# Self attention on one core: units per head, split values, weights streamed pair by pair, row sums inverted on GpSimd

## The reference, cut to what matters

```python
h = rmsnorm(layernorm(x)) * norm_w
q, k, v = h @ w_q, h @ w_k, h @ w_v          # 16 heads of 64
ll = where(tril, q @ k.T / 8, NEG)           # the window is the whole row block of 512
idx = top_k(h @ scorer_w + scorer_b, 128)
lg = where(idx <= pos, q @ k[idx].T / 8, NEG)
attn = softmax(concat([ll, lg]))             # a chosen key counts twice
out = x + (attn @ [v, v[idx]]) @ w_out
```

## Time and profile before

| what | value |
|---|---|
| median of 3 runs | 2299.57 us (2298.17 to 2301.93) |
| profiled execution, its own time | 2303.6 us |
| its span | 2301.9 us |
| mean granted TensorE clock | 0.945 |
| PE / PEld / DVE / ACT / POOL busy in the span | 92% / 72% / 57% / 40% / 15% |
| self attention | from the start to about 1560 us |

### The profile page before, as it was taken

One profiled execution on the slowest core, in us unless ns is written; L12 is line 12 of the kernel. 1 busy time (PEld: TensorE's weight loads), 2 busy tenths in 40 slices (PEclk: granted clock), 3 DMA queues, 4 the chain that ended last, 5 costly groups with the idle time before them and its releaser, 6 DMA issues. The chain is left out here.

```text
span 2301.9 us, 36078 instructions
## 1 busy us (share of the span) xinstructions
PE 2120.8 (92%) x12029; PEld 1654.5 (72%) x12029; DVE 1320.5 (57%) x3145; ACT 930.6 (40%) x1989; POOL 343.7 (15%) x605
## 2 busy tenths in 40 slices
PE   3999999999999999999999999996899999978899
PEld 2886787688588688778868868864788888854543
DVE  5584376178167347537717826743787878745401
ACT  3442344244144244334415414424866666413210
POOL 2100100010010010001001001003554445320000
PEclk9999999999999999999999999996987878769899
DMA  5000000100100100000010010002013212150000
GB/s 192 1 2 33 24 1 13 44 1 1 56 1 1 55 3 1 27 31 1 11 47 1 1 57 1 1 33 81 27 59 133 61 58 67 51 201 1 1 0 19
DMA packets 46137, 80.24 MB, mean 35 GB/s; under 512 B 10067, under 2 KB 10067, under 8 KB 45448
## 3 DMA queue, kind: packets, MB, share of 16 engines
q1 hardware_dynamic: 45320, 75.85, 9.9%
q0 software_dynamic: 640, 2.10, 0.2%
HBM read 60.11 MB, written 17.83 MB: 34 GB/s over the span
## 5 line engine op out<-in xcount | busy, mean ns | idle before, releaser
L403 ACT ACTIVATE probs<-s_bank,nmax 128x512 f32<-128x512 f32 (+3 forms) x512 | 249.5, 526 | 368.5 <-DVE nmax L534 266.4
L686 PE MATMUL o_bank<-vals,probs_t 128*128 128x65 f32 x2560 | 329.0, 272 | 0.1
L686 PEld LDWEIGHTS o_bank<-vals,probs_t 128*128 128x128 f32 x2560 | 312.5, 192 | 13.1 <-DVE probs_t L542 12.9
L534 DVE TENSOR_REDUCE nmax<-s_bank 128x1 f32<-128x512 f32 (+2 forms) x384 | 184.4, 508 | 189.2 <-PE s_bank L663 186.5
L710 PE MATMUL pj_bank<-w_o,o_t 128*128 128x512 f32 x512 | 221.8, 594 | 6.0 <-ACT o_t L411 6.0
L542 DVE COPY probs_t<-pt_bank 128x512 f32<-128x512 f32 x320 | 217.8, 681 | 2.2 <-PE pt_bank L671 2.1
L671 PE MATMUL pt_bank<-ident,probs 128*128 128x128 f32 x1280 | 194.9, 275 | 15.7 <-DVE o_t L449 15.7
L659 PE MATMUL s_bank<-k_twice,q_both 128*128 128x512 f32 (+3 forms) x512 | 190.0, 373 | 2.1 <-DVE k_lo L522 2.1
L710 PEld LDWEIGHTS pj_bank<-w_o,o_t 128*128 128x128 f32 x512 | 96.6, 190 | 126.5 <-issue 126.5
L381 ACT ACTIVATE vals<-pj_bank,twice 128x512 f32<-128x512 f32 x64 | 43.9, 688 | 340.4 <-PE pj_bank L583 334.8
L518 DVE SCALAR_TENSOR_TENSOR q_both<-pj_bank,q_both 64x512 fp32r<-64x512 f32 x128 | 88.1, 688 | 141.7 <-ACT q_both L390 139.1
(11 more groups left out here) (268 smaller groups left out, 4125.3 us busy)
## 6 DMA issues: line engine op xcount, KB each, us to landing
xb<-in_x SPq DMA_DIRECT2D x9, 1024.0 KB, 5.8
xt<-x SPq DMA_DIRECT2D x36, 256.0 KB, 2.8
probs<-in_x SPq DMA_DIRECT2D x32, 256.0 KB, 2.6
x<-probs SPq DMA_DIRECT2D x32, 256.0 KB, 2.0
am<-in_L_ffn_attention_mask SPq DMA_DIRECT2D x8, 1024.0 KB, 5.3
out<-x SPq DMA_DIRECT2D x32, 256.0 KB, 2.5
w_sb<-in_L_ffn_w SPq DMA_DIRECT2D x2, 4096.0 KB, 20.4
o_t<-in_L_attn_w_v SPq DMA_DIRECT2D x2, 1024.0 KB, 9.6
```

Of the source, the lines that this page charges most:

```text
L403: ins = nc.scalar.activation(probs[:, i % 2, c0:c0 + nk], s_bank[i % 2][:, c0:c0 + nk], ACT.Exp, bias=nmax[:, i % 4, n:n + 1])
L534: ins = nc.vector.tensor_reduce(nmax[:, i % 4, n:n + 1], s_bank[i % 2][:, c0:c0 + nk], AX.X, ALU.max, negate=True)
L686: ins = nc.tensor.matmul(o_bank[slot][:, o0:o0 + VW], probs_t[:, i % 2, c0 + P * kt:c0 + P * kt + P], vals[:, kt, 2 * p + h, :], start=(kt ...
```

## The change

Only `self_attention` changes. Cross attention and the feed-forward part stay as they are.

- **Units per head.** Three units for a head (48 a batch): 512 keys; 128 + 384 keys; 256 keys. The mask is no PE product any more: DVE adds it from a tile `masks` while it moves the scores out of PSUM to `probs` (ring of 4) and takes the extreme of the row (one `tensor_tensor_reduce` for a piece). The mask carries -ln 2 for a chosen key, since q is negated. ACT's exponential reads on-chip memory and writes the row sums (`den`).
- **Norm on POOL.** A new step: POOL inverts `den` (power of -1) and multiplies the piece of `probs` by it.
- **Split values and probabilities.** `vals` holds 64 high and 64 low columns per head (fp32r); the turned probabilities are split in `p_hi` (ACT) and `p_lo` (DVE). Per head, PE multiplies 8 times (512, 128, 384, 256 columns, high and low) with `vals` as weights, which gives the result already turned, high part over low part. ACT copies the lower half (`o_raw`), DVE adds (`o`) into `o_t`. The steps `ot` and the reciprocals of L556 are gone.
- **Streamed w_q and w_k.** At the start their split parts are written to HBM (`w_pairs`, 8 MB), and each pair's 1 MB is loaded again in each batch. The second copy of k's high part is moved by a transfer (`move_k`), not by ACT.
- **Slots.** One unit enters in a slot; each later step has its own distance in slots. A projection is cut in thirds of four matmuls, one a slot. Pair 0 of the next batch is projected in the last slots of this one (at the start for batch 0). `dot`, `score` and `rank` stand between the four `out`; `ht` at slots 46 to 49, `stats` at slot 6.

```diff
+STEPS = (("o_raw", 8), ("k_high", 0), ("turned_hi", 3), ("norm", 0), ("s", 0), ("k_lows", 1), ("pv", 8), ("q_high", 0),
+         ("project", 0), ("q_low", 2), ("turned_lo", 4), ("t", 3), ("o", 9))
+AHEAD, LAST_PAIR_AT, HT_AT, STATS_AT = 2, 50, 46, 6
+def unit_rows(u):
+    return ([(3, 0, 512)], [(0, 0, 128), (2, 128, 384)], [(1, 0, 256)])[u]
...
+    plan = [("v", i) for i in range(2 * TT - 1)] + [("tw", 0), ("v", 2 * TT - 1)]
+    for g in range(-AHEAD, LAST_PAIR_AT + 8):
+        for step, behind in STEPS:
+            n = g - behind
+            if step in ("norm", "s", "t", "turned_hi", "turned_lo") and 0 <= n < NU:
+                plan.append((step, n))
+            if step in ("pv", "o_raw", "o") and n >= 0 and n % UNITS == 0 and n // UNITS < NH:
+                plan.append((step, n // UNITS))
...
+    plan += [("out", 0), ("dot", 0), ("out", 1), ("score", 0), ("rank", 0), ("rank", 1), ("out", 2), ("rank", 2),
+             ("rank", 3), ("out", 3)]
...  (POOL)
+                    if kind == "norm":
+                        n = len(unit_rows(i % UNITS))
+                        pl.wait_ge(p_ready, b * NU + i + 1)
+                        step(nc.gpsimd.tensor_tensor(rden[:, i % 4, 0:n], den[:, i % 4, 0:n], minus[:, 0:n], ALU.pow))
+                        for n, (_, c0, nk) in enumerate(unit_rows(i % UNITS)):
+                            part = probs[:, i % RING, c0:c0 + nk]
+                            ins = nc.gpsimd.tensor_tensor(part, part, rden[:, i % 4, n:n + 1].broadcast_to((P, nk)),
+                                                          ALU.mult)
...  (ACT)
+                    if i >= 4:
+                        act.wait_ge(w_stored[1 - i % 2], STORED[1 if i == 4 else 4])
...
             act.wait_ge(split_lo, len(W_ORDER))
+            act.wait_ge(w_stored[1], STORED[5])
...
+                    if kind == "turned_hi":
+                        act.wait_ge(pt_ready, ready)
+                        nc.scalar.copy(p_hi[:, h % 2, TURNED_AT[u], :],
+                                       pt_bank[slot][:, 0:P * n].rearrange("p (n k) -> p n k", k=P)).then_inc(hi_ready, 1)
...  (DVE, step s)
+                        nc.vector.memset(carrier[:, 6 + i % 4:7 + i % 4], 0.0)
+                        for n, (_, c0, nk) in enumerate(unit_rows(i % UNITS)):
+                            ins = nc.vector.tensor_tensor_reduce(
+                                probs[:, i % RING, c0:c0 + nk], s_bank[i % 2][:, c0:c0 + nk],
+                                masks[:, m0 + c0:m0 + c0 + nk], 1.0, 3e38, ALU.add, ALU.min, nmax[:, i % 4, n:n + 1])
...  (DVE, step turned_lo)
+                        nc.vector.tensor_tensor(p_lo[:, h % 2, TURNED_AT[u], :], ... pt_bank ..., p_hi ..., ALU.subtract)
...  (PE)
-                            ins = nc.tensor.matmul(s_bank[slot][:, c0 + nk - P:c0 + nk], ident_b[:, :], causal_b[:, :],
-                                                   start=False, stop=True)
...
+                        parts = [(p, k) for p in (p_hi, p_lo) for k in (0, 3, 1, 2)]
+                        for n, (part, k) in enumerate(parts):
+                            ins = nc.tensor.matmul(o_bank[i % 2][:, 0:P * (TT - k)], vals[:, k, i, :],
+                                                   part[:, i % 2, KEYS_AT[k], :], start=(n == 0),
+                                                   stop=(n == len(parts) - 1))
```

More of the change, by code:

```diff
@@ L85, in attention_plan @@
 def attention_plan():
[L93 to L105, removed]
-            plan.append(("stats", 0))
[L107 to L116, removed]
@@ L117, in attention_plan @@
-    plan.append(("ot", NPAIR - 1))
-    plan += [("out", t) for t in range(TT)]
+    thirds = {}
+    for i in range(1, NPAIR + 1):
+        q0 = 2 * UNITS * (i - 1) - AHEAD if i < NPAIR else LAST_PAIR_AT
+        for j in range(3):
+            thirds[q0 + j] = ("q_third", 3 * i + j)
+            thirds[q0 + 3 + j] = ("k_third", 3 * i + j)
+    last_third = {g: (kind[0], n // 3) for g, (kind, n) in thirds.items() if n % 3 == 2}
+    plan = [("v", i) for i in range(2 * TT - 1)] + [("tw", 0), ("v", 2 * TT - 1)]
@@ new lines, in attention_plan @@
+    for g in range(-AHEAD, LAST_PAIR_AT + 8):
[5 more added lines that the diff above has]
+                plan.append((step, n // UNITS))
+            if step == "project" and g in thirds:
+                plan.append(thirds[g])
+            if step in ("q_high", "q_low", "k_high", "k_lows") and last_third.get(n, " ")[0] == step[0]:
+                plan.append((step, last_third[n][1]))
+        if g == STATS_AT:
+            plan.append(("stats", 0))
+        if HT_AT <= g < HT_AT + DC:
+            plan.append(("ht", g - HT_AT))
@@ L340, in _ @@
             stats(0)
-            with pl.Fori(0, B) as b, done.loop(b, 14 + TT, B):
+            with pl.Fori(0, B) as b, done.loop(b, 14 + TT + NU, B):
                 for r in range(2):
@@ L497, in _ @@
             split(2)
+            split(3)
+            q_low(None, 0)
+            k_lows(None, 0)
             score_row(None, 0)
-            split(3)
+            split(4)
             for t in range(TT):
                 rank(None, 0, t)
-                if t in (1, 3):
-                    split(4 + t // 2)
-            with dv.Fori(0, B) as b, done.loop(b, 2 * TT + 2 * TT + 1 + NU, B):
+                if t == 1:
+                    split(5)
+            with dv.Fori(0, B) as b, done.loop(b, TT + TT + 2 * TT + 1 + 3, B):
@@ L660, in _ @@
                                              start=True, stop=False)
-                            nc.tensor.matmul(s_bank[slot][:, c0:c0 + nk], both, k_lo[:, p % 2, h, 0:nk],
-                                             start=False, stop=False)
-                            ins = nc.tensor.matmul(s_bank[slot][:, c0 + nk - P:c0 + nk], ident_b[:, :], causal_b[:, :],
+                            ins = nc.tensor.matmul(s_bank[i % 2][:, c0:c0 + nk], both, k_low[:, p % 2, h % 2, 0:nk],
                                                    start=False, stop=True)
```

503 lines of the change are left out of this document (301 added, 202 removed).

## The result

The changed kernel takes 2235.92 us (median of 4 runs, 2235.03 to 2236.32) beside 2299.46 (4 runs, 2298.17 to 2301.93) for the kernel before on the same chip: ratio 0.972, 95% interval 0.9705 to 0.9739. It is 2.8% faster. The forecast was 2132, the range 2060 to 2220; the time lies 16 us above the range. The profiled execution of the changed kernel takes 2235.0 us, of which its span is 2233.0.

What follows compares the result with a forecast made beforehand. PE was taken to bound self attention: 157 floor + 5 stall + 2 clock + 3 coupling = 167 us a batch, 22.8 less; 2303.6 - 8 x 22.8 + 14.5 = 2135.7, forecast as 2132 for the median; range 2060 to 2220.

Steps and rivals of the forecast that it cites:

- in the batch above the granted clock is full: Clock term: full clock in the old kernel's batch read; after the new 5 us wait, about 2 us a batch lost.
- PE's floor: PE's summed work in a self-attention batch: 157 us against 189.7, with 6.48 us a head in the units.
- rival 4: DVE's `tensor_tensor_reduce` at half rate: about 2390 us, or 2292 without the gaps; chance 0.06.
- above 90%: Sign for the changed profile: DVE's busy share in the units stretch, from 6.3 us a head against PE's 6.5.
- Rival 3: POOL blocked by DVE's new operations in the units: 10.4 us a head, about 2600 us; chance 0.04.
- `stats` and the clock: POOL's `stats` at slot 6 delays norm 7, so PE stands 5 us a batch; lower clock then costs 2.
- Coupling: PE, DVE and ACT in order at near paces with few slots between them: 3 us a batch, bounds 0 and 10.
- rival 2: DVE and ACT set the units' pace, DVE at 7.1 us a head: batch about 178.5, 2224 us; chance 0.25.
- rivals 1 and 2: First: no stall of note, batch 159, 2068 us, chance 0.20; second: DVE and ACT set the pace, chance 0.25.
- the last pair's projection now covers that drain: End of the units: the old order's wait for the last `ot` and its copy goes, covered by projection work.
- The start: Before the loop: sixth weight half split only after the fifth is stored; 14.5 us later, ends +8 and +25.
- three things that "would make the forecast wrong": PE waiting for POOL every slot; 512-column reduce over 0.9 us; values-product matmuls over 0.25 us for 512 columns.

Runs made afterwards that it cites:

- e6: e5 with one more POOL product of 96 columns for each norm, which nothing reads: 2133.12 us, ratio 0.9275.
- e7: e5 with one more POOL product of 512 columns for each norm, which nothing reads: 2345.2 us, ratio 1.0201.
- e1: Changed kernel with the step `stats` after the fourth value step instead of at slot 6: 2179.17 us, ratio 0.9447.
- e3: Changed kernel with the `ht` steps inside the loop writing to the projection banks, not the units' transpose banks: 2181.4 us, ratio 0.947.
- e12: e5 with PE's and ACT's `ht` at slots 45 to 48 and DVE's low part a slot later, 46 to 49: 2093.7 us, ratio 0.9101.
- e5: Changed kernel with `stats` after the fourth value step, `ht` in the projection banks, the fifth weight half's parts in the values' tile at the start: 2113.19 us, ratio 0.9196.

## Why the prediction was wrong

The direction, the floor and the named stall were right; the batch was 10.5 us too short. The profiled 2235.0 less the forecast sum of 2135.7 is 99.3 us:

| where | us over the forecast | how |
|---|---|---|
| start | 5.1 | third value step 69.24 against 49.67: 19.6 later, 14.5 put in the sum |
| batch 0, from there | 14.3 | 184.4 to 175.9, 8.5 less instead of 22.8 |
| batches 1 to 6 | 72 | 188.35 to 177.5 each, 10.8 less instead of 22.8 |
| batch 7 | 10.4 | 188.3 to 175.9 |
| after attention | -2.7 | 749.4 to 746.7 |

The remaining 0.2 is rounding and the time around the span. Of the 12 us a batch, 1.45 lie in the kernel before: the sum starts from 189.8, and six of its batches take (1364.18 - 234.09)/6 = 188.35. The batch that I read, 422.17 to 611.86, is 1.6 us longer than its neighbours, though PE waits in it as in them. In each of the eight batches PE waits 1.96 us for `o_t`; in the one read, and in the last, the granted clock then was lower for the next 4 us, and in the six others it was not. So "in the batch above the granted clock is full" does not hold for these 4 us. PE's rows in the kernel before, then the 4 us after the wait in the batch read and in the next:

```profile
234.09 0.50 PE L581 MATMUL pj_bank<-wv_hi,ht_hi 128*128 128x512 f32 x1 [0.87 <-DVE probs L574]
...
512.65 0.63 PE L671 MATMUL pt_bank<-ident,probs 128*128 128x128 f32 x4 [1.96 <-DVE o_t L449]
...
702.38 0.63 PE L671 MATMUL pt_bank<-ident,probs 128*128 128x128 f32 x4 [1.96 <-DVE o_t L449]
...
1364.18 0.50 PE L581 MATMUL pj_bank<-wv_hi,ht_hi 128*128 128x512 f32 x1 [0.87 <-DVE probs L574]
```

```profile
512.60:516.60 4.00, 3.95 (x25) 3.57 (x25) 2.97 (x6) 1.53 (x3) 0.00 (x0) 0.71 0.01 4
702.40:706.40 4.00, 4.00 (x31) 3.61 (x32) 3.25 (x8) 1.53 (x3) 0.00 (x0) 1.00 0.02 4
```

The other 10.5 are all in the stretch of the units. Term by term:

- **PE's floor, right.** A head takes 6.41 us where nothing waits, forecast 6.48. The first stage takes 24.2, of which eight matmuls of q and k are 1.8 (8 x 0.229), so 22.4, forecast 22.5; `out` takes 29.1, forecast 29.07. From `p_hi` to `p_lo` the values product takes 0.64 us (303.15 to 303.79), 1.3 a head, as forecast.
- **DVE, right in price, too high in share.** The reduce takes 0.691 us at 512 columns (0.69 forecast), so rival 4 is out. Where nothing waits, 297 to 360 us, DVE is busy 51.97 of 63, 82%, where "above 90%" stood: 5.3 us a head (0.825 x 6.41) and not 6.3. Its records of that stretch add up to 58.9 us, because most start 0.06 to 0.09 us before the one ahead of them ends; I had added durations.

```profile
297.00:360.00 63.00, 62.89 (x367) 54.30 (x367) 51.97 (x158) 50.94 (x132) 44.05 (x69) 0.99 0.26 84
```

- **ACT, not a bound, as forecast.** Busy 50.94 of 63, 5.2 us a head, a little under the 5.5 to 5.9 of the forecast. The read of the accumulator overlaps both neighbours, so it costs 0.09 us net (from a read's start to the next instruction's, 322.34 to 322.43), the dear end of the 0 to 0.1 forecast.
- **POOL, at its low end.** The power takes 0.54 (one column) and 0.70 (two), as forecast, a 512-column product 1.04, not 1.25. A head is 4.7 us by its records (2 x 0.54 + 0.71 + 2.88), forecast 5.6. With e6's 1.3 a head more PE's pitch still holds where heads follow each other, with e7's 3.3 more it doesn't. Rival 3, the blocked POOL, did not come: the products keep their 1.041 us while DVE, busy 82% of that stretch, reads PSUM and one on-chip tile. The Trainium skill (SBUF — State Buffer, Who interferes with whom) states that a VectorE instruction with at most one on-chip input, outside its 2-port modes, does not contend with GpSimd; the trace agrees.
- **`stats` and the clock, right.** 5 + 2 forecast, e1 gives 6.9. The wait is 4.32, for norm 7 as forecast, and the clock is at 0.54 in the 2 us after it.
- **Coupling, not where it was put.** 3 us (0 to 10) were forecast for three engines near one pace. The pitch of 6.41 has no room for it, since DVE and ACT stand at 5.3 and 5.2; what couples the three engines is the drain, below. The heads ran into no second bound, so rival 2, whose 2224 is nearest to the result, is near in the number and wrong in the cause. The range stopped at 2220, short of this rival, which had a chance of 0.25. (The chance of "faster", 0.92, is also 0.02 more than the forecast and rivals 1 and 2 add up to.)
- **The failed step: "the last pair's projection now covers that drain".** The stretch of the units takes 102.5 + 21.7 + 1.8 = 126.0 us, 13.6 more than the floor's 105.5 and the 6.9 of `stats`, and for these nothing was put down but the 3 of the coupling. The projection does not cover the drain's waits: its thirds come at slots 50 to 55, from 386.53 on, after PE's four waits of 1.0 to 2.3 us. I priced `ht` as 1.8 us of PE work. Its place was not priced: it takes every second one of two banks, between transposes, while PE has the least else to do, and its low part stands ahead of `p_lo` in DVE's queue. e3 shows 6.8 us a batch for the banks, e12 2.0 for the queue (with PE's and ACT's part a slot sooner, which no run has alone). e3's 6.8 include what the lower clock cost (0.76 over the drain of the changed kernel), which no run parts from the waits; in e5's drain the clock is at 1.00. The other 4.9 (161.9 in e12 less the floor of 157) are open. In e12 PE's waits come to 4.2 us a batch, all under 1.5, of which the floor holds 1.4; no run names a place for the rest.
- **The start, right in kind.** The chain was as walked: the sixth half is split only after the fifth is stored from the same tile. The walk ends at 62 to 63, which is 13 to 14 after 48.93, not the 14.5 of the sum. ACT's first value copy came at 67.9. The fifth half was split at 46.0 (44 forecast), stored by 55.9 (51), the sixth split at 60.7 (56) and stored by 67.9: the splits take about the 5 us that were walked, the stores 9.9 and 7.2 instead of some 7.

None of the three things that "would make the forecast wrong" happened. The list asked whether an engine or an instruction is slower than thought, and not what order the steps have where the pipeline empties.

## What to carry to other kernels

A step that is cheap in work can be dear in place: before a plan is priced, follow each ring of buffers and each engine's queue through the last slots, where nothing covers a wait, and ask for each instruction at the head of a queue what stands behind it. Give different chains different banks, and put the second half of a two-engine step one slot behind the first: that gained 6.8 and 2.0 us a batch here, at no cost in work. When the fill of one engine is doubtful, add work to it in an experiment (e6, e7): two runs showed here that 1.3 us a head more on POOL leave the pitch of the heads as it is and cost 2 us a batch at its end, and that 3.3 are too many. Size a period on several repetitions, not one. And where a view names a releaser, ask whether the program waits for it (e5's POOL row).

## What the runs showed of the hardware

- Reading ACT's accumulator was an instruction of its own, 191 ns in the mean of 512 records after four widths (97.9 us), 0.09 us net from start to start. DVE's took 0.08 us and started together with the next instruction, so it cost nothing net.
- A GpSimd product with a broadcast column took 1041, 827, 613 and 400 ns for 512, 384, 256 and 128 columns: 1.67 ns a column and 0.19 us fixed, less than the 2.42 of the two-tile row. The Trainium skill (GPSIMD Engine Reference, Performance versus the Vector engine) gives 2.6 cycles a column at 1.2 GHz for two tensor inputs; the 2.0 cycles here are lower, and the measurement decides for this form.
- After a wait of 4.3 us the granted clock was at 0.54 in the next 2 us, and four matmuls of the values product took 1.35 instead of 0.80 us. In the drain it fell in the 2 us from 376, during the third of four waits (1.00, 1.09, 2.31 and 2.25 us), and was at 0.50 from 378 to 387. In e5, whose waits there are of 1.46 us and less, it stayed at 1.00 (336 to 350).
- The same wait did not always bring the clock down: after eight equal waits of 1.96 us in the kernel before, one a batch, it was at 0.71 over the next 4 us in two batches and at 1.00 in the six others. The units of the two took 1.6 us longer. What made the difference is not known.
